# A four-layer gated block on one core: value products ahead of the last row sums, row pieces copied one by one, half of a rectified product on VectorE, and a new table of steps

## The reference

```python
x = x + tanh(g_xattn[1]) * mlstm(ln(x), ctx, ctx, Wi, bi, Wf, bf, ln_scale)       # stage A below: decays from running sums
x = x + tanh(g_xattn[2]) * attention_with_cache(ln(x), ctx, wq, wk, wv, wo)       # "2" steps: keys2 .. mix2
x = x + tanh(g_ffn[2])   * bitnet_swiglu(ln(x), w_gate, w_up, w_down)             # "2" steps: in2a .. out2
x = x + tanh(g_xattn[3]) * memory_attention_top54(ln(x), W_qkv, W_o, ctx, ctx)    # "3" steps: queries3 .. project3
# the last part:
def _L3_ffn_ref(x, w1, w2):
    h = bitlinear(x, w1)              # activations rounded to 8 bits, weights to -1, 0, 1
    h = jnp.square(jax.nn.relu(h))
    return bitlinear(h, w2)           # quantised again by the largest element of each row
x = x + tanh(g_ffn[3]) * _L3_ffn_ref(ln(x), w1, w2)
```

## Time and profile before

| what | us |
|---|---|
| median of 3 runs (lowest, highest) | 565.84 (562.04, 568.44) |
| the profiled execution | 569.39 |
| its span (first to last instruction) | 567.7 |
| PE / DVE / ACT / POOL busy in the span | 461.2 / 355.7 / 234.0 / 145.7 |
| mean granted TensorE clock, share of full speed | 0.901 |

### The profile page before, as it was taken

How to read it: one execution, slowest core, us unless ns; L and a number is a source line. 1 busy time by engine, 2 the same in 40 slices (tenths; PEclk the granted TensorE clock), 3 DMA queues, 4 the chain that set the end, 5 groups by cost and what they waited for, 6 DMA issues and landing times.

```text
span 567.7 us, 7522 instructions
## 1 busy us (share of the span) xinstructions
PE 461.2 (81%) x2709; PEld 339.5 (60%) x2718; DVE 355.7 (63%) x987; ACT 234.0 (41%) x422; POOL 145.7 (26%) x139
## 2 busy tenths in 40 slices
PE   1899989999999837779889689999887754766775
PEld 0688875557787625445556457788664533654544
DVE  6473456639314546695656668246478899799753
ACT  1200013532242715354543212423888643225896
POOL 4000010064854675433064555001000000010000
PEclk9999987999899968777798689999999996897978
DMA  8840260025894410001000200000000000000001
GB/s 269 273 186 1 72 224 1 1 68 193 307 286 133 145 53 17 7 5 38 0 1 2 76 1 1 1 0 1 0 2 0 1 1 0 2 1 0 10 29 38
DMA packets 21078, 34.70 MB, mean 61 GB/s; under 512 B 4935, under 2 KB 16074, under 8 KB 21040
## 3 DMA queue, kind: packets, MB, share of 16 engines
q1 hardware_dynamic: 18736, 30.23, 15.8%
q0 software_dynamic: 2304, 3.97, 2.5%
HBM read 32.32 MB, written 4.19 MB: 64 GB/s over the span
## 4 chain that ended last, share of the span: by engine, by line
PE 46%; DVE 30%; ACT 11%; POOL 6%; issue 5%; DMA 1%; DVEq 0%; POOLq 0%; ACTq 0%
PE bank L1516 5%; PE bank L1475 5%; PE bank L1485 5%; PE bank L1592 4%; PE bank L1847 3%; PE bank L1861 2%; DVE bnst L613 2%; DVE HN L623 2%; PE bank L1614 2%; DVE top L1137 2%; POOL ar L568 2%; DVE big L1134 2%; PE bank L1668 2%; DVE am L1019 2%; DVE X L824 1%
## 5 line engine op out<-in xcount | busy, mean ns | idle before, releaser
L471 POOL TENSOR_TENSOR rstd<-ve,neghalf 128x2 f32<-128x2 f32 x32 | 23.3, 729 | 270.0 <-DVE ve L618 269.9
L954 DVE TENSOR_TENSOR SH<-bank,HM 128x512 f32<-128x512 f32 x32 | 21.8, 688 | 23.2 <-ACT HM L1315 10.6
L1315 ACT ACTIVATE HM<-bank 128x512 f32<-128x512 f32 x32 | 19.1, 597 | 36.5 <-PE bank L1701 29.3
L623 DVE TENSOR_SCALAR HN<-X,mv,rstd 128x256 f32<-128x256 f32 x64 | 28.6, 488 | 7.8 <-POOL rstd L471 7.6
L1592 PEld LDWEIGHTS bank<-ph,big 128*128 128x128 f32 x256 | 31.9, 196 | 1.3 <-issue 0.4
L1475 PE MATMUL bank<-HM,CT 128*128 128x256 f32 x128 | 30.7, 403 | 1.2 <-DVE HM L647 1.2
L568 POOL TENSOR_TENSOR ar<-ar,neghalf 128x32 f32<-128x32 f32 x4 | 21.7, 5432 | 38.7 <-DVE ar L918 38.7
L1516 PE MATMUL bank<-HT,SH 128*128 128x512 f32 x64 | 31.6, 645 | 0.0
L1592 PE MATMUL bank<-ph,big 128*128 128x64 f32 x256 | 31.2, 276 | 0.0
L1475 PEld LDWEIGHTS bank<-HM,CT 128*128 128x128 f32 x128 | 26.0, 204 | 5.6 <-issue 1.5
L613 DVE BATCH_NORM_STATS2 bnst<-X 128x6 f32<-128x256 f32 x64 | 24.0, 418 | 7.6 <-POOL X L580 6.8
(11 more groups left out here) (364 smaller groups left out, 1160.7 us busy)
## 6 DMA issues: line engine op xcount, KB each, us to landing
big<-in_ew SPq DMA_DIRECT2D x16, 768.0 KB, 6.5
y_rows<-ph SPq DMA_DIRECT2D x16, 128.0 KB, 3.2
X<-in_x SPq DMA_DIRECT2D x4, 256.0 KB, 6.7
CT<-in_ctxT SPq DMA_DIRECT2D x1, 1024.0 KB, 7.7
CN<-in_ctx SPq DMA_DIRECT2D x1, 1024.0 KB, 11.4
ar<-in_q2g SPq DMA_DIRECT2D x1, 1024.0 KB, 4.9
ar<-in_q2u SPq DMA_DIRECT2D x1, 1024.0 KB, 7.1
big<-in_q2d SPq DMA_DIRECT2D x1, 1024.0 KB, 10.1
```

What stands on the lines that cost most here:

```text
L471: pool.tensor_tensor(rstd[:, b, :], ve[:, b, :], neghalf[:, 0:TB], ALU.pow)\
L623: last = dve.tensor_scalar(HN[:, TB * b + j, :], X[:, TB * b + j, :], mv[:, b, j, 0:1], rstd[:, b, j:j + 1], ALU.subtract, ALU.mult)
L954: dve.tensor_tensor(cs[:, g, :], bank[i % 3][:], dcs[:, i % 2, :], ALU.mult).then_inc(s["s_cs"], 1)
L1315: act.activation(dcs[:, i % 2, :], bank[4 + i % 2][:], ACT.Exp).then_inc(s["s_dexp"], 1)
```

## The change

1. TensorE makes the four `VC` products directly behind the four before them, ahead of `last_sums` and of the first `tokens_turn`; ScalarE copies them there too. Two waits that had been met already are dropped.
2. VectorE: `token_norm(0)` and `gathered(2)` move ahead of `weight_scales(4, 5)`, and `gathered(3)` moves behind `part_rows(0)`.
3. `part_rows` signals each piece, and `compose_rows` copies each piece as it comes.
4. `rows_turn(0)` on TensorE, `spread_rows(0)` and `turned_rows(0)` on ScalarE move behind the first round's exponents, scores and decays; `weighted_values(0)` moves from round 0 to round 1.
5. In the last part the second 512 columns are rectified on VectorE (a multiplication with a maximum), the first on ScalarE. The square (ScalarE) and the largest element (VectorE) become a step of their own, `max3`, which the table can place.
6. All four strings of `TURNS_OF` are new.

```diff
-        (("in3", "TVS"), ("round3", "S"), ("turn3", "TS"), ("out3", "TV"))]
+        (("in3", "TVS"), ("max3", "VS"), ("round3", "S"), ("turn3", "TS"), ("out3", "TV"))]
-    "G": ("2223031323012301230123"),
+    "G": ("2220331320132301201323"),
...
             def part_rows(r):
-                link(dve.tensor_copy(part[p0:p1, 0, :], CG[p0:p1]))
+                dve.tensor_copy(part[p0:p1, 0, :], CG[p0:p1]).then_inc(s["s_part"], 1)
+                dve.wait_ge(s["s_part"], 3 * r + 1)
                 link(dve.tensor_tensor(rest[p0:p1], CG[p0:p1], part[p0:p1, 0, :], ALU.subtract))
-                link(dve.tensor_copy(part[p0:p1, 1, :], rest[p0:p1]))
+                dve.tensor_copy(part[p0:p1, 1, :], rest[p0:p1]).then_inc(s["s_part"], 1)
+                dve.wait_ge(s["s_part"], 3 * r + 2)
...
             ln_stats(0)
+            token_norm(0)
+            gathered(2)
             dve.wait_ge(s["s_gc"], 1)
             weight_scales(4, 5)
-            token_norm(0)
-            gathered(2)
             gate_rows(0)
-            gathered(3)
             sum_rows(0)
             max_rows(0)
             part_rows(0)
+            gathered(3)
             ln_stats(1)
...
-                if i in (0, 9, 18, 23):
-                    weighted_values((0, 9, 18, 23).index(i))
+                if i in (1, 9, 18, 23):
+                    weighted_values((1, 9, 18, 23).index(i))
...
                 if step[0] == "in3":
-                    dve.wait_ge(s["s_gs"], nth("S", INS, step, b))
+                    dve.wait_ge(s["s_gu"], nth("T", INS, step, b))
+                    dve.tensor_scalar(GS[b][:, 512:1024], bank_b(b)[:], fg[:, TB * b + step[1], 0:1], 0.0, ALU.mult,
+                                      ALU.max).then_inc(s["s_gv"], 1)
+                if step[0] == "max3":
+                    dve.wait_ge(s["s_gv"], nth("V", IN3, ("in3", step[1]), b))
+                    dve.wait_ge(s["s_gs"], nth("S", INS, ("in3", step[1]), b))
                     hidden_scale(b, 1)
...
             for h in range(2):
                 magnitudes(4, h)
+            for b in range(B):
+                folded(2 + B + b, VC[b])
...
             def compose_rows(b):
-                act.wait_ge(s["s_part"], min(b, 2) + 1)
                 for p in range(3):
+                    act.wait_ge(s["s_part"], 3 * min(b, 2) + p + 1)
                     last = act.activation(CMP[32 * p:32 * (p + 1), b, :], part[32 * b:32 * (b + 1), p, :], ACT.Copy)
...
             log_rows(0)
-            for b in range(B):
-                folded(2 + B + b, VC[b])
             compose_rows(0)
-            spread_rows(0)
-            turned_rows(0)
             for i in range(4 * NO):
                 decays(i)
+                if i == 0:
+                    spread_rows(0)
+                    turned_rows(0)
...
                 if step[0] == "in3":
                     act.wait_ge(s["s_gu"], nth("T", INS, step, b))
-                    for n in range(2):
-                        last = act.activation(GS[b][:, 512 * n:512 * (n + 1)], bank[2 * b + n][:], ACT.Relu,
-                                              scale=fg[:, TB * b + step[1], 0:1])
-                    last.then_inc(s["s_gs"], 1)
+                    act.activation(GS[b][:, 0:512], bank_a(b)[:], ACT.Relu, scale=fg[:, TB * b + step[1], 0:1])\
+                        .then_inc(s["s_gs"], 1)
+                if step[0] == "max3":
+                    act.wait_ge(s["s_gs"], nth("S", INS, ("in3", step[1]), b))
+                    act.wait_ge(s["s_gv"], nth("V", IN3, ("in3", step[1]), b))
                     act.activation(H[b], GS[b], ACT.Square).then_inc(s["s_sq"], 1)
```

More of the change, by code:

```diff
@@ L399, in flamingo @@
         IN3 = [("in3", j) for j in range(TB)]
-        FULL = [("in2b", j) for j in range(TB)] + IN3
+        MAX3 = [("max3", j) for j in range(TB)]
+        FULL = [("in2b", j) for j in range(TB)] + MAX3
         INS = IN2 + [("in3", j) for j in range(TB)]
@@ L1420, in _ @@
                     if step[0] == "round3":
[L1421 to L1422 removed]
+                        act.wait_ge(s["s_sq"], nth("S", MAX3, ("max3", step[1]), b))
+                    act.wait_ge(s["s_rh"], nth("V", FULL, ("in2b" if step[0] == "round2" else "max3", step[1]), b))
                     act.activation(H[b], H[b], ACT.Identity, bias=magic[:, 0:1], scale=rh1[:, b:b + 1])\
```

25 lines of the change are left out of this document (11 added, 14 removed).

## The result

| | before | change |
|---|---|---|
| median of four runs each, on one chip | 563.98 us | 548.59 us |
| lowest and highest | 562.04, 568.44 | 547.18, 553.61 |
| ratio, with its 95% interval | | 0.9719 (0.9657 to 0.9782) |
| profiled execution / its span | 569.39 / 567.7 | 547.58 / 545.7 |

Two later comparisons on other chips, with six executions of the change each, gave 554.24 against 568.61 (ratio 0.9798, 0.9728 to 0.9867) and 555.16 against 568.07 (0.9748, 0.9686 to 0.9810). By medians and ratios these are 11.5 to 14.4 us, so that 12 to 14 us is the better figure for its worth, and both medians lie inside the range that I gave.

What follows compares the result with a forecast made beforehand. The prediction saw handovers limiting stage A, no full engine from 401, VectorE in the clips, ScalarE behind the last one. Gains 3.0 + 2.0 + 5.0 = 10.0 us off a median of 565.84 gave 556 us, range 549 to 566.

Steps and rivals of the forecast that it cites:

- A: From the weight products ahead of every edit to the loop's last two products on VectorE; forecast 3.0 us gained.
- B: From the loop's last two products on VectorE to the last clip's last MATCH_REPLACE; forecast 2.0 us gained, 0.3 lost.
- C: From the last clip's last MATCH_REPLACE to the last addition's end; the forecast 5.3 us counted from that clip's start.
- So L1668 stays at 3.27 us: Stage A: moving the products ahead doesn't speed up the first gates, which stay at the 1.2 GHz price.
- The table, 2.0: 327 to 452 us: two fewer table loads and batch 3's later place bring scores3(b0) 2.0 us sooner, bounds 0 and 4.
- the 4 of the layout: Both tables' first steps laid out: scores3(b0) about 4 us sooner, no handovers between engines counted; half was taken.
- The clips, +0.3: From scores3(b0) to the last clip: 2.7 us new VectorE work less a 2.37 us wait, so 0.3 us later.
- Behind the last clip, 5.3: Last clip's start to last addition's end: ScalarE relieved, VectorE loaded; 48.5 instead of 54.2 us, 5.3 taken.
- the 35 of my sign: Expected evidence: 48 to 50 us from the last clip's start to the last addition, ScalarE busy below 35 us.
- (1): VectorE becomes the limit of the end through 5.5 us of new work; no gain there, 561 us; chance 0.18.
- (2): The new table only passes waits on between engines; only stage A's gain stays, about 563 us; chance 0.12.
- (3): GpSimd's power of batch 3 lies exposed behind the variance of lowout1(b0), up to 13 us, about 569; chance 0.10.

Runs made afterwards that it cites:

- e5: The change itself, unaltered, run again on another chip against the kernel before: 554.24 against 568.61 us, ratio 0.9798.
- e1: Items 1 to 4 of the change alone (stage A) on the kernel before: 564.35 against 567.93 us, ratio 0.9936.
- e4: The change with both halves of the rectification on ScalarE again: 555.98 us against 567.93 for the kernel before, ratio 0.9791.
- e14: The change with both rectification halves on ScalarE, run beside the unaltered change: 559.69 us against 568.07 for the kernel before, ratio 0.9776.
- e15: The change with only the rectification of in3(b1,j0) put back on ScalarE: 552.07 us against 568.07 for the kernel before, ratio 0.9688.
- e2: Item 1 alone (the four VC products moved ahead) on the kernel before: 567.88 against 567.93 us, ratio 0.9974.
- e13: The change itself, unaltered, run once more against the kernel before: 555.16 against 568.07 us, ratio 0.9748.
- e6: Item 5 alone (half rectification on VectorE, old order of steps) on the kernel before: 571.96 against 568.61 us, ratio 1.0081.
- e11: The change with in3(b1,j0) behind the last clip on VectorE instead of ahead: 561.44 us against 567.70 for the kernel before, ratio 0.9874.
- e9: The new table of steps with the maximum as its own step, nothing else, on the kernel before: 555.61 against 567.70 us, ratio 0.9846.

## Why the prediction was right or wrong

**The sum.** Forecast were 3.0 for A, 2.0 less 0.3 for B, and 5.3 for C with the last clip. In the change's first profile it was 5.6, 3.8 and 6.1; over three executions 4.8, 2.8 and 6.1. The three mechanisms came as forecast; each term was sized too small, and one of them, A, by a step that was wrong. The first comparison was lucky besides: its profile had the early gathers, gates of 1.91 us and the shortest low1 of the change's three, which makes 1.8 us against their mean (15.5 and 13.7).

**Stage A, 3.0.** The failing step is "So L1668 stays at 3.27 us". I read a clock of 0.52 behind a wait of 3.9 us and gave the first gates the same, although the wait ahead of them would shrink, from 7.5 to 2.2 us (3.5 with the late gathers). It went both ways: 1.91 us in two executions of the change, 3.51 in the third (e5), 3.20 to 3.54 in e1, e4, e14 and e15. And the transposes ahead of the gates, which I had left as they were, took 0.65 or 0.66 us in every execution with the products ahead, where they took 1.09 in every other. So the gate rows, which I held at 212.31, start 6.6 us behind the end of tile 1's additions where the gates took 1.91 us and 7.6 to 8.0 where they took 3.2 to 3.54; it was 8.6 to 8.9. The chain behind them was right: 3.6 us from pieces and exponents as worked out, 3.5 measured from gate rows to exponents. That the products cost nothing alone (e2) and that moving token_norm(0) gives nothing were right too: from the end of tile 1's additions to the norm are 2.45 us before and in e1. With gates of 3.2 us the term is near what I took: 3.6 by e1's times, 4.1 by its trace against others with early gathers. The rest of the 5.6 is the shorter gates (0.6, from A of e1 and e4 against that of the change and e13) and the form of the gathers (1.0, from A before, 126.64, against 125.65).

**The table, 2.0.** ScalarE's first `in2a` work came as said, with six table loads and five of them in the stretch of 375 to 452 (groups of ScalarE there):

```profile
L1419 ACT ACT_TABLE_LOAD x3 | 3.8, 1283 | 0.1
L1398 ACT ACT_TABLE_LOAD x1 | 1.3, 1283 | 0.0
L1451 ACT ACT_TABLE_LOAD x1 | 1.3, 1283 | 0.0
```

in2a(b0,j0) on TensorE starts at 379.02; counted from the mark it moved from 209.5 to 195.8, 13.7, of which 5.6 came from stage A: 8.1 against my 7. scores3(b0) stands 132.73 us behind the loop's end where it stood 135.79 (451.83 - 316.04): 3.1 gained, between the 2.0 that I took and the 4 of the layout: halving it was no reading of a row. In e5 and e13 the first clip starts 0.7 and 1.1 us later, so that 2 to 3 us is the worth. The loads cost 1283 ns with no idle time around them; the drain that the Trainium skill, "ScalarE: Activation LUTs", section What ACT_TABLE_LOAD costs, adds does not appear in the rows after either.

**The clips, +0.3.** They became 0.8 us shorter: from scores3(b0) to the last clip's first MATCH_REPLACE 58.63 us instead of 59.38. VectorE's idle time in this stretch fell from 5.0 of 59.3 us to 1.7 of 58.6. I had counted only the one wait of 2.37; the rest went as well. In e13, with a granted clock of 0.66 around the first clip instead of 0.79, 1.2 us of it are lost again. The new rectification took 0.75 us, the upper end of my bounds (the Trainium skill, "VectorE: DVE Perf Modes", section The TRN2 errata, would give some 0.66 as an estimate for 512 elements out of PSUM; the row decides).

**Behind the last clip, 5.3.** From the last clip's start (495.61) to the last addition's end (543.63) are 48.0 us; I had 48.5 by the layout and took off 0.4 for a clock of 0.89, which rose to 0.96. ScalarE is 35.36 us busy in it, just above the 35 of my sign; before it was 44.22, and my 40.41 had left out the time under the clip. In C it fell by 8.2 us to 32.66, near the fall that I had laid out (40.41 to 31.8).

**The base.** I took the change off a median of three, 565.84. In the later comparisons the median of before was 567.7 to 568.6, so that my base was some 2 us low; that the later medians of the change come within 2 us of my 556 is in part this error, which hides the undersized terms. The first comparison, on the other hand, probably drew the shorter early part more often for the change (three of its four executions lie within 547.2 to 549.6), which the later medians of 554.2 and 555.2 did not.

**The rivals.** (1) VectorE as the limit of the end: with the new order it has no wait above 0.6 us between 504 and 537.8, so it and ScalarE are both full, but 6.1 us were gained all the same. In the old order the rival is what happened (e6, +3.4 us). I had priced it at zero gain, not at a loss, and hadn't seen that the in3 ahead of the last clip is what keeps it away in the change (e11). (2) The table does nothing: fell, 8 us with e9. (3) GpSimd's power: it lies as laid out. The last rows of GpSimd's work on batch 3 and the waits that follow, after:

```profile
340.65 1.26 POOL L582 TENSOR_TENSOR X<-X,ar 128x512 f32<-128x512 f32 x1
342.02 0.75 DVE L615 BATCH_NORM_STATS2 bnst<-X 128x6 f32<-128x256 f32 x2 [4.96 <-POOL X L582]
345.82 0.66 PE L1468 MATMUL bank<-identf,HN 128*128 128x128 f32 x4 [0.28 <-DVE HN L625]
```

The addition ends at 341.91, which is the 354.1 of my layout less the 12.2 us by which this execution is ahead there (low1 at 315.39 instead of 327.65 makes 12.3); TensorE stands 0.28 us. "No slack" was right to a quarter of a microsecond, and no exposure came.

**What stays open.** A and B of the same kernel differ by 2 us from execution to execution because of three draws that the rows show: the form of the gathers (1.7 us between the change's first profile and e5), the clock of the first gates, and TensorE's clock in B, where low1 took 8.53, 8.81 and 10.16 us (after, e5, e13) and the stretch around the first clip was granted 0.79, 0.77 and 0.66. Why a draw falls as it does stays open. So does whether the rectification on VectorE is worth its 2.0 us by the times.

## What to carry to other kernels

Work that is moved to a second engine is paid for at its place in that engine's queue: the same eight rectifications gave 2.0 us by the traces in one order and took 3.4 us by the medians in the other, because two of them stood behind a clip of 10.7 us. Before counting how much an engine is relieved, look up what it will wait for, and what stands ahead of that. Where a clock can fall either way ahead of a serial chain, price both cases and give both a chance, and count both kernels from a mark ahead of every edit, and look for work that differs without an edit, so that a draw isn't put down to the change.

## What the runs showed of the hardware

With the same wait of TensorE ahead (2.22 and 2.21 us) the same eight products ran at 2.4 GHz in one execution (1.91 us, granted clock 1.00) and fell to 1.2 GHz under way in another (3.20 us, 0.57 in the mean). Filling the waits kept the clock for the first gates and exponents only: batch 1's gates took 2.76 us with them filled and 2.80 (e13) and 2.92 without. A rectification of 512 columns out of PSUM on VectorE, with one scalar for each row, takes 0.75 us, as much as a product of two tensors and such a scalar (0.746), while ScalarE does the same in 0.69.
